# A two-part graph network on one core: loads of layer 2's counts in seven pieces, of the edge attributes in four, and an earlier first zero fill

## The chip, the core and the metric

One core of a Trainium2 chip runs the whole program. The metric is the time of the device in microseconds (us). The kernel before took 3525.62 us (median of three runs, 3514.42 to 3532.14).

## What is computed

There are 6250 nodes with 64 features and 206250 edges, sorted by destination. Two graph networks follow each other, each with a residual and a layer norm.

```python
def _sage_conv(x, src, dst, W_l, b_l, W_r):
    agg = segment_sum(x[src], dst) / maximum(count(dst), 1)[:, None]
    return agg @ W_l + b_l + x @ W_r
# first network
h = relu(_sage_conv(x, src, dst, W_l1, b_l1, W_r1))
h = relu(_sage_conv(h, src, dst, W_l2, b_l2, W_r2))
x = layernorm(x + h @ W_out + b_out)
# second network
m = selu(concat([x[src], edge_attr], 1) @ W1a + b1a) @ W1b + b1b
mean = segment_sum(m, dst) / maximum(count(dst), 1)[:, None]
x = layernorm(x + selu(concat([x, mean, u[0]], 1) @ W2a + b2a) @ W2b + b2b)
```

## The kernel before

The engines work side by side. Each has its own list of instructions, and semaphores tie the lists together: an instruction or a transfer raises one when it is done, and a `wait_ge` holds up everything behind it in the same list. The transfers that SP starts go out in the order of SP's list.

**Layer 1, about 0 to 670 us.** The nodes are cut into 14 superblocks of 448. For each of them TensorE and VectorE build the matrix of edge counts from every source (49 blocks of 128) to the 448 destinations, as 128 x 49 x 448 values of 16 bits, in one of the two halves of `A_sb`. TensorE multiplies the features with it, and SP stores it in DRAM (`A_d`, 5488 KB each, line 564). SP also fills the rows of `sorted_edges` with zeros, in eight pieces called `blank(r)` (lines 566 to 569, 1716 KB each), one behind each of the superblocks 4 to 11 (lines 576 to 579). The weights are loaded near the start (lines 534 to 547). The vector `zrow` of zeros is set by GpSimd in its first instructions.

**Layer 2, about 670 to 1280 us.** TensorE's `sums2(s)` (line 1408) computes the sums for one superblock from the counts and the stored features of layer 1: a product with zeros (line 1411) that opens the sum, a wait for the counts (line 1415), then seven bodies of 21 products (line 1435), each followed by one step `layer2(m, b)` of the superblock before it (line 1445). The steps are, in this order: turning the old features (`hT_turned`) and the product with `Wl2`; the product with `Wr2` (`v2_ready`); turning the new features (`h2_turned`); the product with `Wout` (`o_ready`); nothing; turning the normalised rows; and the last products (`pq_ready`). After the bodies 1, 3 and 6 there is also one small step of a sort (`place_group`). `agg2_ready` is raised by the last product of body 6, ahead of that body's `layer2` step. The counts of superblocks 12 and 13 are still on the chip when layer 2 begins, so `sums2(0)` and `sums2(1)` use those. The others, `sums2(2)` to `sums2(13)`, use twelve matrices that SP loads back, alternately into the two halves of `A_sb`.

SP's part is `superblock2(s)` (line 615):

```python
def superblock2(s, half, at_before=None):
    sp.wait_ge(agg2_ready, s)
    if s < NSB - 1:
        sp.dma_start(A_sb[:, 1 - half, :], A_d[...s - 1...]).then_inc(A_in[1 - half], 16)   # L618
    sp.wait_ge(x2_ready, s + 1)
    ...load_hx(s, half)                                                                    # L607, L608
    sp.wait_ge(p_ready, s)
    sp.dma_start(by_node(p_d, ...), pc[:, :, :]).then_inc(p_stored, 16)                    # L626
```

So the load in `superblock2(s)` is for `sums2(s + 1)`, and `p_ready` is raised to `s` by VectorE's last instruction for the superblock that `sums2(s)` carries with it (line 1944), which reads what TensorE wrote just ahead of `sums2(s + 1)`.

Between the bodies the first 40 groups of 1024 edges are sorted: ScalarE's queue loads them (`load_group`, lines 1062 to 1070), VectorE finds their places (`sort_group`, `slot_group`), and GpSimd writes their rows to `sorted_edges` with eight indirect transfers a group (line 890).

**The edges, about 1280 to 3526 us.** The other 162 groups go through the network in their own order. For group `h`, SP loads the attributes (`load_attr`, line 701, 256 KB, one of six buffers, 128 partitions of 2 KB), GpSimd gathers the source terms with eight indirect transfers (line 915), TensorE turns the attributes (`turn_attr`, line 1513, transposes of line 1519), multiplies them (line 1527) and sums the messages (line 1535), and VectorE and ScalarE compute the selu between them. Mixed in are 104 units of 512 sorted edges. SP loads a unit with two transfers (`load_unit`, lines 715 and 716), and TensorE turns it (`turn_unit`, line 1538, last transpose of line 1545). SP's list has the unit's two loads directly behind a `load_attr`, and `turn_unit` comes one group later in TensorE's list than the `turn_attr` for which that `load_attr` waited.

Of the kernel before, what the change touches and what calls it, by code (L numbers as in the profile page):

```python
# [7 lines left out]
F32 = mybir.dt.float32  # L8
# [8 lines left out]
P = 128  # L17
N = 6250
E = 206250
F = 64  # L20
# [23 lines left out]
SBN = SB_GROUPS * GROUP  # L44
NSB = 14
PAIRS = NSB // 2
BODIES = 7
BG = SB_GROUPS // BODIES
BH = SRC_BLOCKS // BODIES
# [9 lines left out]
EG = 1024  # L59
# [3 lines left out]
WIN = 48  # L63
RING = 3
DEEP = 6

RG = 5
NR = 8
PG = RG * NR
NEGC = NEG - PG  # L70
# [27 lines left out]
CELL_TILES = [cell_tiles(r) for r in range(NR)]  # L98
# [54 lines left out]
def build(nc, x, src, dst, edge_attr, Wl1, bl1, Wr1, Wl2, bl2, Wr2, Wout, bout,  # L153
# [8 lines left out]
    A_d = dram("counts_matrix", [NSB, P, SRC_BLOCKS * SBN], FP16)  # L162
# [6 lines left out]
    sorted_d = dram("sorted_edges", [NTILES * P + PRING * EG, F + 2], F32)  # L169

    with ExitStack() as ctx:
# [10 lines left out]
        A_sb = sb("A_sb", [P, 2, SRC_BLOCKS * SBN], FP16)  # L182
# [44 lines left out]
        zrow = sb("zrow", [P, 512], BF16)  # L227
# [163 lines left out]
        iota_set = sem("iota_set")  # L391
# [90 lines left out]
        def by_node(t, m):  # L482

            return t[bass.ds(m * SBN, SBN), :].rearrange("(c q) f -> q c f", q=CH)
# [34 lines left out]
        def _(sp):  # L519
# [26 lines left out]
            for half in range(2):  # L546
                sp.dma_start(Wedge[half * F:(half + 1) * F, half * F:(half + 1) * F], W1a[F:2 * F, :]).then_inc(w2_in, 16)

            def store_h(m, half):
                sp.wait_ge(h_split, m + 1)  # L550
                sp.dma_start(by_node(h1_d, m), hs[:, :, :]).then_inc(h_stored, 16)
                for part in range(3):
                    sp.dma_start(by_node(hp_d[part], m), hpart[:, part, :, :]).then_inc(h_stored, 16)
# [9 lines left out]
                sp.wait_ge(counts_moved, (s + 1) * SB_GROUPS + 2)  # L563
                sp.dma_start(A_d[bass.ds(s, 1), :, :].rearrange("a p n -> (a p) n"), A_sb[:, half, :]).then_inc(A_stored[half], 16)

            def blank(r):
                n, top = sum(CELL_TILES[r]), sum(sum(t) for t in CELL_TILES[:r])
                sp.dma_start(sorted_d[top * P:(top + n) * P, :].rearrange("(p t) f -> p (t f)", p=P).rearrange("p (t f) -> p t f", f=2 * (F + 2)),
                             zrow[:, 0:4 * (F + 2)].bitcast(F32).unsqueeze(1).to_broadcast([P, n // 2, 2 * (F + 2)])).then_inc(pm_blank, 16)

            for s in range(4):
                superblock(s, s % 2)
            sp.wait_ge(iota_set, 10)
# [1 line left out]
                sp.dma_start(pm_dst[:, :], dst[0:PG * EG].rearrange("(r q) -> r q", q=RG * EG)[:, 0].partition_broadcast(P)).then_inc(pm_dst_in, 16)  # L575
            for s in range(4, NSB):
                superblock(s, s % 2)
                if s - 4 < NR:
                    blank(s - 4)
            sp.wait_ge(xT_ready, NSB - 2)  # L580

# [30 lines left out]
            sp.wait_ge(A_stored[0], 16 * PAIRS)  # L612
            sp.wait_ge(A_stored[1], 16 * PAIRS)

            def superblock2(s, half, at_before=None):
                sp.wait_ge(agg2_ready, s)
                if s < NSB - 1:
                    sp.dma_start(A_sb[:, 1 - half, :], A_d[bass.ds(s - 1, 1), :, :].rearrange("a p n -> (a p) n")).then_inc(A_in[1 - half], 16)  # L618
                sp.wait_ge(x2_ready, s + 1)
                if isinstance(s, int) and s == 1:  # L620
                    sp.dma_start(h1m[1][:, :, :], by_node(h1_d, NSB - 1)).then_inc(hx_in[1], 16)
                    last_rows(xm[:, 1], hx_in[1])
                else:
                    load_hx(s, half)
                sp.wait_ge(p_ready, s)
                sp.dma_start(by_node(p_d, s - 3 if at_before is None else at_before), pc[:, :, :]).then_inc(p_stored, 16)  # L626

            superblock2(1, 1, NSB - 2)
            superblock2(2, 0, NSB - 1)
# [71 lines left out]
            def load_attr(h):  # L701
                g, k = PG + h, h % DEEP
                if h >= DEEP:
                    sp.wait_ge(attr_turned, h - DEEP + 1)
                if g < gE:
                    sp.dma_start(attr[k], edge_attr[g * EG:(g + 1) * EG, :].rearrange("(p j) f -> p (j f)", p=P)).then_inc(attr_in[k], 16)
                    return
                sp.dma_start(attr[k][0:ETAIL // EJ, :], edge_attr[te:te + ETAIL // EJ * EJ, :].rearrange("(p j) f -> p (j f)", j=EJ)).then_inc(attr_in[k], 16)
                sp.dma_start(attr[k][ETAIL // EJ:ETAIL // EJ + 1, 0:ETAIL % EJ * F], edge_attr[te + ETAIL // EJ * EJ:E, :].rearrange("(p j) f -> p (j f)", p=1)).then_inc(attr_in[k], 16)
# [528 lines left out]
        def _(pe):  # L1238
# [169 lines left out]
            def sums2(s, half, m=None):  # L1408
                if s > 0:
                    pe.wait_ge(agg2_moved, s)  # L1410
                pe.matmul(agg_ps[:, 0:SBN], zrow[:, 0:P], zrow[:, 0:SBN], start=True, stop=False, skip_group_check=True)
                if s < 2:
                    pe.wait_ge(counts_moved, NSB * SB_GROUPS + 2)
                else:
                    pe.wait_ge(A_in[half], s // 2 * 16)
                if s == 0:

                    for part in (2, 0, 1):
                        pe.wait_ge(part_in[part], 16)
                        for blk in range(EARLY):  # L1420
                            pe.matmul(agg_ps[:, 0:SBN], Hsb[:, part, blk, :], Asb(half)[:, blk, :], start=False, stop=True, skip_group_check=True)
                        if part == 0:
                            place_group(0)
                    pe.wait_ge(parts_in, 48)
                    for blk in range(EARLY, SRC_BLOCKS):
                        for part in range(3):
                            ins = pe.matmul(agg_ps[:, 0:SBN], Hsb[:, part, blk, :], Asb(half)[:, blk, :], start=False, stop=True, skip_group_check=True)
                    ins.then_inc(agg2_ready, 1)
                    return
                for b in range(BODIES):  # L1430
                    if s == NSB - 1 and b == BODIES - 1:
                        turn_last()
                    for blk in range(b * BH, (b + 1) * BH):
                        for part in range(3):
                            ins = pe.matmul(agg_ps[:, 0:SBN], Hsb[:, part, blk, :], Asb(half)[:, blk, :], start=False,  # L1435
                                            stop=(part == 2), skip_group_check=True)
                    if b == BODIES - 1:
                        ins.then_inc(agg2_ready, 1)
                    if s == NSB - 1 and b == BODIES - 1:
                        last_terms()  # L1440
                    layer2(m, b, 1 - half)
                    if b in (1, 3, 6):
                        place_group(3 * s - BEFORE + (1, 3, 6).index(b))
# [68 lines left out]

            def turn_attr(h):
                k = h % DEEP
                pe.wait_ge(attr_in[k], 16 * (h // DEEP + 1) + (16 if h == NEGC - 1 else 0))
                if h >= 1:
                    pe.wait_ge(attr_moved, h)
                for c in range(EJ // 2):
                    ins = pe.transpose(t_ps[:, c * P:(c + 1) * P], attr[k][:, c * P:(c + 1) * P], ident[:, :])  # L1519
                ins.then_inc(attr_turned, 1)  # L1520
# [707 lines left out]
```

## Time and profile before

| | |
|---|---|
| median of 3 runs | 3525.62 us |
| the profiled execution's own time | 3528.27 us |
| its span, first to last instruction | 3526.4 us |
| mean granted clock of TensorE, share of full | 0.768 |
| TensorE (PE), products | 2255.4 us busy, 64% |
| GpSimd (POOL) | 1785.5 us busy, 51% |
| VectorE (DVE) | 1420.1 us busy, 40% |
| ScalarE (ACT) | 962.0 us busy, 27% |

The page shows one execution. A busy share is the mean over stages that are bound differently, so the stages have to be read one at a time. "Landing" is the time from a transfer's issue to the semaphore that tells of its end. A wait put down to "remote" or to "another core or an unknown queue" is one whose releaser the profile couldn't name; there is one core here.

### The profile page before, as it was taken

The page shows a single profiled execution, that of the slowest core. Times are in us where ns is not written, and L with a number is a line of the kernel's source. Part 1 is how long each engine was busy: PE and PEld are TensorE (multiplying, and loading weights), DVE is VectorE, ACT ScalarE, POOL GpSimd, SP SyncE. Part 2 cuts the span into 40 slices and gives each one's busy share as a digit, 9 for nine tenths or more (in the row PEclk, how much of TensorE's full clock was granted, in tenths as well). Part 3 has the DMA queues.
Part 4 walks back from the last instruction along what each step waited for, and adds up shares of the span by engine and source line. Part 5 has one row for each costly group of instructions (what it writes and reads, how often), then busy time and mean ns, then how long its engine had stood idle before and what let it go on. Part 6 is the DMA issues. An engine that isn't in the chain of part 4 may idle for free.

```text
span 3526.4 us, 49813 instructions
## 1 busy us (share of the span) xinstructions
PE 2255.4 (64%) x17118; PEld 1609.5 (46%) x17118; DVE 1420.1 (40%) x2775; ACT 962.0 (27%) x2094; POOL 1785.5 (51%) x1840
## 2 busy tenths in 40 slices
PE   1799999888888851556556645555565555553543
PEld 1456555444444431444445444444544444443533
DVE  5698888143333340333323323232332323231323
ACT  2677777100000021222212212122222212221222
POOL 6233222155555556555555555555555555555562
PEclk9999999989988965676667767667666766665566
DMA  6346776678454411322212212222122222221111
GB/s 226 142 151 203 221 224 184 184 154 234 167 175 168 145 58 43 86 45 51 47 41 49 50 41 50 44 49 47 45 49 45 49 47 46 48 47 39 39 39 33
DMA packets 408743, 335.34 MB, mean 95 GB/s; under 512 B 296503, under 2 KB 357256, under 8 KB 404859
## 3 DMA queue, kind: packets, MB, share of 16 engines
q1 hardware_dynamic: 299249, 262.08, 25.2%
q0 software_dynamic: 54368, 57.24, 7.1%
q10 hardware_dynamic: 54922, 13.25, 1.8%
q8 instruction: 134, 2.20, 0.3%
q14 instruction: 70, 0.57, 0.1%
HBM read 199.25 MB, written 133.06 MB: 94 GB/s over the span
## 4 chain that ended last, share of the span: by engine, by line
PE 39%; another core or an unknown queue 29%; issue 18%; ACT 4%; DVE 4%; DMA 2%; SPq 1%; POOL 1%; DVEq 1%; ACTq 0%; POOLq 0%
PE agg_ps L1435 5%; PE cnt_ps L1306 5%; PE cnt_ps L1527 4%; PE agg_ps L1312 4%; PE agg_ps L1313 4%; PE u_ps L1566 3%; PE agg_ps L1576 3%; PE agg_ps L1535 3%; PE u_ps L1562 2%; PE t_ps L1519 2%; DMA overlapping_rows<-A_sb 1%; POOL A_sb L915 1%; SPq L637 1%; ACT A_sb L1137 1%
## 5 line engine op out<-in xcount | busy, mean ns | idle before, releaser
L915 POOL DMA_INDIRECT A_sb<-source_terms,src_cur x1296 | 1242.1, 958 | 950.9 <-ACT src_cur L1125 580.7
L1535 PE MATMUL agg_ps<-A_sb 128*65 128x48 f32 x2592 | 267.2, 253 | 361.4 <-issue 285.4
L1748 DVE TENSOR_TENSOR arena<-iota_code,arena 128x2048 f16<-128x2048 f16 (+1 forms) x392 | 435.8, 1178 | 79.9 <-PE cnt_ps L1306 67.4
L890 POOL DMA_INDIRECT sorted_edges<-pm_row,pm_to x320 | 315.0, 984 | 299.6 <-DVE pm_to L1898 210.1
L1435 PE MATMUL agg_ps<-A_sb,arena 128*128 128x448 f16 x1911 | 410.0, 367 | 43.3 <-issue 40.5
L1535 PEld LDWEIGHTS agg_ps<-A_sb 128*65 128x65 f32 x2592 | 244.1, 172 | 402.7 <-issue 314.4
L1010 ACT ACTIVATE A_sb<-cnt_ps 128x392 f32 (+1 forms) x784 | 385.7, 497 | 151.7 <-PE cnt_ps L1306 79.7
L1527 PE MATMUL cnt_ps<-Wedge,A_sb 128*128 128x128 f32 x1296 | 278.5, 363 | 176.3 <-issue 129.8
L1158 ACT ACTIVATE A_sb<-u_ps 128x256 f32<-128x256 f32 x104 | 40.1, 385 | 1072.1 <-remote 769.3
L1527 PEld LDWEIGHTS cnt_ps<-Wedge,A_sb 128*128 128x128 f32 x1296 | 235.1, 261 | 200.7 <-issue 153.4
L1566 PE MATMUL u_ps<-arena 128*128 128x64 bf16 x2472 | 172.6, 211 | 232.5 <-issue 231.7
L2055 DVE TENSOR_TENSOR A_sb<-A_sb,agg_ps 65x48 f32 (+1 forms) x266 | 67.8, 255 | 604.9 <-remote 452.9
L1306 PE MATMUL cnt_ps<-arena 128*128 128x98 f16 x3136 | 282.0, 214 | 42.6 <-ACT A_sb L1010 30.4
L1435 PEld LDWEIGHTS agg_ps<-A_sb,arena 128*128 128x128 bf16 x1911 | 188.8, 101 | 236.0 <-issue 90.8
L1306 PEld LDWEIGHTS cnt_ps<-arena 128*128 128x128 f16 x3136 | 189.5, 101 | 230.8 <-issue 183.3
L1566 PEld LDWEIGHTS u_ps<-arena 128*128 128x128 bf16 x2472 | 140.8, 111 | 253.7 <-issue 247.8
L1131 ACT ACTIVATE A_sb<-t_ps 128x512 f32<-128x512 f32 x162 | 96.4, 595 | 556.7 <-remote 385.6
L1313 PE MATMUL agg_ps<-A_sb,arena 128*65 128x448 f16 x686 | 243.9, 356 | 0.0
L1312 PE MATMUL agg_ps<-A_sb,arena 128*128 128x448 f16 x686 | 243.5, 355 | 0.2 <-ACT A_sb L1010 0.2
L2078 DVE SCALAR_TENSOR_TENSOR A_sb<-u_ps,A_sb 128x256 f32<-128x256 f32 x104 | 43.9, 422 | 446.9 <-ACT A_sb L1160 399.9
L2037 DVE TENSOR_TENSOR cnt_ps<-cnt_ps,A_sb 128x512 f32<-128x512 f32 x162 | 112.0, 691 | 120.9 <-remote 113.9
L817 POOL DMA_INDIRECT arena<-overlapping_rows,start_row x26 | 38.6, 1483 | 221.7 <-DVEq L1725 217.3
(295 smaller groups left out, 3222.4 us busy)
## 6 DMA issues: line engine op xcount, KB each, us to landing
counts_matrix<-A_sb SPq DMA_DIRECT2D x14, 5488.0 KB, 16.4
A_sb<-counts_matrix SPq DMA_DIRECT2D x12, 5488.0 KB
arena<-in_edge_attr_dram SPq DMA_DIRECT2D x107, 256.0 KB
A_sb<-source_terms,src_cur POOLq DMA_INDIRECT x1296
A_sb<-in_edge_attr_dram SPq DMA_DIRECT2D x54, 256.0 KB
sorted_edges<-zrow SPq DMA_DIRECT2D x8, 1716.0 KB, 25.2
arena<-sorted_edges SPq DMA_DIRECT2D x104, 128.0 KB
overlapping_rows<-A_sb SPq DMA_DIRECT2D x1, 13056.0 KB
```

The lines of the kernel that those rows point to most:

```text
L890: pool.indirect_dma_start(out=sorted_d, out_offset=bass.IndirectOffsetOnAxis(ap=pm_to[:, k, j:j + 1], axis=0), in_=pm_row[:, k, j, :], in_ ...
L915: pool.indirect_dma_start(out=gath[k][:, j * F:(j + 1) * F], out_offset=None, in_=p_d, in_offset=bass.IndirectOffsetOnAxis(ap=src_cur[k][: ...
L1010: act.activation(Asb(half)[:, :, bass.ds((b * BG + k) * GROUP, GROUP)].rearrange("p b (w j) -> p b w j", j=PAIR), cnt_ps[k % 2][:, 0:SUB * ...
L1306: ins = pe.matmul(cnt_ps[k % 2][:, c * CODES:(c + 1) * CODES], lane_hot[:, at + c // 2, :, c % 2], code_hot[:, at + c // 2, :, c % 2], sta ...
L1312: pe.matmul(agg_ps[:, 0:SBN], X12[:, blk, :], rhs, start=(blk == 0), stop=(blk == SRC_BLOCKS - 1), skip_group_check=True)
L1313: ins = pe.matmul(agg3_ps[0:F + 1, 0:SBN], X3[:, blk, :], rhs, start=(blk == 0), stop=(blk == SRC_BLOCKS - 1), skip_group_check=True)
L1435: ins = pe.matmul(agg_ps[:, 0:SBN], Hsb[:, part, blk, :], Asb(half)[:, blk, :], start=False, stop=(part == 2), skip_group_check=True)
L1527: ins = pe.matmul(cnt_ps[h % 2][:, c * P:(c + 1) * P], attrT[h % RING][:, c * P:(c + 1) * P], Wedge[:, :], start=True, stop=True)
L1535: ins = pe.matmul(agg3_ps[0:F + 1, 0:WIN], msg[h % RING][:, j, :], hot[h % RING][:, j, :], start=(j == 0), stop=(j == EJ - 1))
L1566: ins = pe.matmul(u_ps[:, j * F:(j + 1) * F], lane_p[u % 2][:, a, j * P:(j + 1) * P], P3[:, 2 * b + a, part, :], start=False, stop=(part = ...
L1748: ins = dve.tensor_tensor(hot_rows[:, slots], iota_code[:, 0:n, :].unsqueeze(1).to_broadcast([P, AT_ONCE * SUB // 2, n, 2]), turned[:, bas ...
L2037: dve.tensor_tensor(cnt_ps[h % 2][:, 0:EJ * F], cnt_ps[h % 2][:, 0:EJ * F], gath[h % DEEP], ALU.add).then_inc(z_made, 1)
```

## The change

Three things are changed. SP's load of a counts matrix becomes seven transfers of 784 KB (49/7 = 7 source blocks each). Piece 0 stands where the whole load stood, and pieces 1 to 6 stand behind the store of line 626, each of them behind a wait for the piece before it (`16 * i` on `A_in`) and in groups behind waits for `hT_turned`, `v2_ready`, `h2_turned` and `o_ready`. TensorE waits for all seven. The load of a group's attributes becomes four transfers of 32 partitions (64 KB); from the seventh group on each waits for the one before it. The first zero fill moves from behind superblock 4 to behind the weights.

```diff
+QUARTERS = 4
+QP = P // QUARTERS
+A_PARTS = BODIES
...
             for half in range(2):
                 sp.dma_start(Wedge[half * F:(half + 1) * F, half * F:(half + 1) * F], W1a[F:2 * F, :]).then_inc(w2_in, 16)
+            def blank(r):
+                ...
+            sp.wait_ge(iota_set, 10)
+            blank(0)
...
             for s in range(4, NSB):
                 superblock(s, s % 2)
-                if s - 4 < NR:
+                if 1 <= s - 4 < NR:
                     blank(s - 4)
...
+            def load_counts(s, half, i):
+                if s == NSB - 1:
+                    return
+                if i > 0:
+                    sp.wait_ge(A_in[half], 16 * A_PARTS * ((s - 1) // 2) + 16 * i)
+                cols = slice(i * BH * SBN, (i + 1) * BH * SBN)
+                sp.dma_start(A_sb[:, half, cols], A_d[s - 1, :, cols]).then_inc(A_in[half], 16)
+
             def superblock2(s, half, at_before=None):
                 sp.wait_ge(agg2_ready, s)
-                if s < NSB - 1:
-                    sp.dma_start(A_sb[:, 1 - half, :], A_d[bass.ds(s - 1, 1), :, :].rearrange("a p n -> (a p) n")).then_inc(A_in[1 - half], 16)
+                load_counts(s, 1 - half, 0)
                 sp.wait_ge(x2_ready, s + 1)
...
                 sp.wait_ge(p_ready, s)
                 sp.dma_start(by_node(p_d, s - 3 if at_before is None else at_before), pc[:, :, :]).then_inc(p_stored, 16)
+                sp.wait_ge(hT_turned, s)
+                load_counts(s, 1 - half, 1)
+                load_counts(s, 1 - half, 2)
+                sp.wait_ge(v2_ready, s)
+                load_counts(s, 1 - half, 3)
+                sp.wait_ge(h2_turned, s)
+                load_counts(s, 1 - half, 4)
+                load_counts(s, 1 - half, 5)
+                sp.wait_ge(o_ready, s)
+                load_counts(s, 1 - half, 6)
...
                 if g < gE:
-                    sp.dma_start(attr[k], edge_attr[g * EG:(g + 1) * EG, :].rearrange("(p j) f -> p (j f)", p=P)).then_inc(attr_in[k], 16)
+                    whole_rows = edge_attr[g * EG:(g + 1) * EG, :].rearrange("(p j) f -> p (j f)", p=P)
+                    for q in range(QUARTERS):
+                        if q > 0 and h >= DEEP:
+                            sp.wait_ge(attr_in[k], 16 * QUARTERS * (h // DEEP) + 16 * q)
+                        sp.dma_start(attr[k][q * QP:(q + 1) * QP, :], whole_rows[q * QP:(q + 1) * QP, :]).then_inc(attr_in[k], 16)
                     return
...
-                    pe.wait_ge(A_in[half], s // 2 * 16)
+                    pe.wait_ge(A_in[half], s // 2 * 16 * A_PARTS)
...
-                pe.wait_ge(attr_in[k], 16 * (h // DEEP + 1) + (16 if h == NEGC - 1 else 0))
+                pe.wait_ge(attr_in[k], 16 * QUARTERS * (h // DEEP) + 16 * (2 if h == NEGC - 1 else QUARTERS))
```

## Rows read from the trace of the kernel before

**Rows 1.** Busy time by stretch, in us: start:end length, then each engine's busy time.

```profile
957.50:1002.00 44.50, 36.64 (x199) 20.50 (x198) 17.31 (x57) 2.77 (x6) 23.60 (x24) 0.88 0.51 174
...
1500.00:3150.00 1650.00, 944.44 (x7523) 770.99 (x7522) 512.83 (x969) 363.37 (x868) 914.73 (x959) 0.69 0.21 47
```

**Rows 2.** Timeline of SP's queue in layer 2: start us, us, line, transfer.

```profile
696.51 0.37 SPq L618 DMA_DIRECT2D A_sb<-counts_matrix  x1
...
731.12 0.33 SPq L626 DMA_DIRECT2D source_terms<-iota_i  x1
731.49 0.49 SPq L618 DMA_DIRECT2D A_sb<-counts_matrix  x1
...
1002.41 0.33 SPq L626 DMA_DIRECT2D source_terms<-iota_i  x1
1002.78 0.49 SPq L618 DMA_DIRECT2D A_sb<-counts_matrix  x1
...
1220.45 0.33 SPq L626 DMA_DIRECT2D source_terms<-iota_i  x1
```

**Rows 3.** Timeline of TensorE where two superblocks of layer 2 begin.

```profile
827.90 2.42 PE L1435 MATMUL agg_ps<-A_sb,arena 128*128 128x448 f16 x6 [2.12 <-DMA A_sb<-counts_matrix]
...
1001.60 0.53 PE L1411 MATMUL agg_ps<-zrow 128*128 128x448 bf16 x1
...
1001.92 5.60 PE L1435 MATMUL agg_ps<-A_sb,arena 128*128 128x448 f16 x21
```

**Rows 4.** Chain that ended last, at the one load of counts on it.

```profile
810.87 16.67 DMA A_sb<-counts_matrix
```

**Rows 5.** DMA issues of the page: count, KB each, median us to landing.

```profile
counts_matrix<-A_sb SPq DMA_DIRECT2D x14, 5488.0 KB, 16.4
...
sorted_edges<-zrow SPq DMA_DIRECT2D x8, 1716.0 KB, 25.2
...
h_rows<-hs SPq DMA_DIRECT2D x14, 224.0 KB, 2.6
...
out_dram<-arena SPq DMA_DIRECT2D x13, 112.0 KB, 2.3
...
out_dram<-arena SPq DMA_DIRECT2D x1, 84.0 KB, 1.8
```

**Rows 6.** Timeline at the start: a load of 803.2 KB and the instruction it releases.

```profile
2.30 0.45 SPq L521 DMA_DIRECT2D A_sb<-in_dst_dram  x1
...
7.20 0.25 DVE L1682 CAST A_sb<-A_sb 128x102 int16<-128x102 int32 x1 [5.70 <-DMA A_sb<-in_dst_dram]
```

**Rows 7.** Timeline of GpSimd and ScalarE in one superblock of layer 2.

```profile
995.64 0.97 POOL L890 DMA_INDIRECT sorted_edges<-pm_row,pm_to  x1 [0.30 <-issue]
998.96 0.54 ACT L1085 ACTIVATE agg3S<-cnt_ps 64x448 f32<-64x448 f32 x1 [16.70 <-remote]
...
1009.36 6.97 ACTq L1070 DMA_DIRECT2D pm_ends<-in_dst_dram  x1
...
1020.12 0.97 POOL L890 DMA_INDIRECT sorted_edges<-pm_row,pm_to  x1 [5.26 <-DVE pm_to L1898]
```

**Rows 8.** Timeline of the edges, SP's queue: loads of a group and of a unit.

```profile
1961.94 0.35 SPq L706 DMA_DIRECT2D arena<-in_edge_attr_dram  x1
1962.33 0.43 SPq L715 DMA_DIRECT2D arena<-sorted_edges  x1
1962.81 0.51 SPq L716 DMA_DIRECT2D arena<-sorted_edges  x1
...
2015.62 0.35 SPq L706 DMA_DIRECT2D arena<-in_edge_attr_dram  x1
```

**Rows 9.** The same stretch: TensorE's turning of units, and ScalarE's waits.

```profile
1968.75 0.27 PE L1545 MATMUL t_ps<-ident,arena 128*8 128x128 f32 x1
...
1976.61 2.08 PE L1527 MATMUL cnt_ps<-Wedge,A_sb 128*128 128x128 f32 x8 [5.40 <-issue]
...
2023.19 0.27 PE L1545 MATMUL t_ps<-ident,arena 128*8 128x128 f32 x1
...
2043.35 0.39 ACT L1158 ACTIVATE A_sb<-u_ps 128x256 f32<-128x256 f32 x1 [16.78 <-PE u_ps L1566]
```

**Rows 10.** Timeline near 74 us: the last weights, and the gathers behind them.

```profile
71.66 2.22 SPq L547 DMA_DIRECT2D Wedge<-in_L_gnn_W1a_dram  x2
...
100.40 0.94 POOL L801 DMA_INDIRECT arena<-first_dst,part_of  x1 [0.30 <-issue]
...
104.54 0.89 ACT L1010 ACTIVATE A_sb<-cnt_ps 128x392 f32 x2 [4.47 <-remote]
```

More of the change, by code:

```diff
@@ L547, in _ @@
                 sp.dma_start(Wedge[half * F:(half + 1) * F, half * F:(half + 1) * F], W1a[F:2 * F, :]).then_inc(w2_in, 16)
+            def blank(r):
+                n, top = sum(CELL_TILES[r]), sum(sum(t) for t in CELL_TILES[:r])
+                sp.dma_start(sorted_d[top * P:(top + n) * P, :].rearrange("(p t) f -> p (t f)", p=P).rearrange("p (t f) -> p t f", f=2 * (F + 2)),
+                             zrow[:, 0:4 * (F + 2)].bitcast(F32).unsqueeze(1).to_broadcast([P, n // 2, 2 * (F + 2)])).then_inc(pm_blank, 16)
+            sp.wait_ge(iota_set, 10)
+            blank(0)
             def store_h(m, half):
@@ L564, in superblock @@
                 sp.dma_start(A_d[bass.ds(s, 1), :, :].rearrange("a p n -> (a p) n"), A_sb[:, half, :]).then_inc(A_stored[half], 16)
[L566 to L569, printed above, removed]
             for s in range(4):
```

## The prediction

> **What bounds the kernel now.** I first read the busy time by stretch. No engine is full in either of the stages that the change touches. One superblock of layer 2 takes 44.5 us with TensorE busy for 36.6 and GpSimd for 23.6, and in the 1650 us of the edges TensorE is busy for 944 and GpSimd for 915 [rows 1]. So each stage is a loop of waits, and what counts is which wait ends last.
>
> In layer 2 the load of the counts is not that wait. SP issues it within 1.2 us of the start of a superblock: line 626, behind which it stands, goes out at 1002.41, the load at 1002.78, and TensorE opened the sums at 1001.60 [rows 2, 3]. It lands about 16.7 us later [rows 4] and is needed only at the next superblock, some 44 us on. What costs time there is elsewhere: ScalarE sits idle for 16.7 us, until just after GpSimd has written the last of a run of 16 row transfers [rows 7]. The edges show the same picture, with ScalarE idle for 16.8 us at a time [rows 9]. Only once is a load of counts waited for, for 2.12 us at 827.90 [rows 3], where it had been queued behind the long index loads.
>
> **Layer 2, the term that decides.** The seven pieces would have to be on the chip before `sums2(s + 1)` begins. Piece 0 is: it keeps the old place. Pieces 1 to 6 stand behind SP's wait for `p_ready` at `s`. That semaphore is raised when superblock `s` is completely done, and the rows show when this is: line 626, the first thing behind the wait, goes out at 1002.41, while TensorE's first product that needs counts ran at 1001.92 [rows 2, 3]. So pieces 1 to 6 begin 0.5 us after the moment at which all seven are wanted. The four new waits (`hT_turned`, `v2_ready`, `h2_turned`, `o_ready`) spread nothing, because each asks for a step of `sums2(s)`, and all of these came before `p_ready`. They cost nothing either. Nothing else can be in front: the matrix that was loaded in the 44 us of cover now has one seventh of its load in that cover.
>
> What remains is six transfers, one after the other, since each waits for the landing of the one before. The price of one (784 KB): a transfer of 224 KB lands in 2.6 us [rows 5] and one of 5488 KB in 16.67 [rows 4]. On the line between them 784 KB takes 2.6 + 560 x (16.67 - 2.6)/5264 = 4.1 us. I add 0.1 for SP to wake and issue the next, and take 4.2. The bounds are 2.6 (the smaller transfer) from below and 4.9 from above, from the load of 803.2 KB issued at 2.30 that releases VectorE at 7.20, next to another load of its size [rows 6]. I choose near the upper one because its size is nearly the same.
>
> The Trainium skill's page "DMA: Bandwidth & Descriptors", section "Anatomy of one DMA — SWDGE (gpsimd) path", puts one transfer at about 2.0 us plus its bytes over 436 GB/s, which would make a piece 3.8 us, an estimate from that page; its section "Bandwidth" tells to batch transfers to 1 MiB or more, which speaks against cutting this load. With 3.8 in place of 4.2 the sum below would be 29 us less.
>
> Per superblock: SP's store of line 626 and the gap, 0.37; six pieces, 25.2; and 0.49 from TensorE's first product to line 626. That is 26.1 us in which TensorE stands still. VectorE and ScalarE soon stand as well, since their steps hang on products of the same superblock, and GpSimd has one group of eight writes to do (some 10 us) and then waits. Nothing covers it. It comes 12 times, for `sums2(2)` to `sums2(13)`: line 626 goes out 12 times between 731.12 and 1220.45 [rows 2]. 12 x 26.1 = 313 us. The wait of 2.12 us at 827.90 [rows 3] is inside it, so 311. With the bounds of the piece it is 196 to 361.
>
> What comes back? Piece-wise loading lets other queues in between. In the trace an issue of ScalarE's queue took 6.97 us while the whole matrix was loading [rows 7]. But the places that GpSimd waits for at 1020.12 come from VectorE [rows 7], behind TensorE's bodies, so the writes start no earlier. I book nothing, and keep 0 to 40 us for the range.
>
> **The edges.** TensorE waits for the attributes of a group that were asked for six groups earlier, so the four quarters themselves are hidden. What is queued behind them is not: a unit's two loads. Today they go out 0.4 and 0.9 us behind line 706 [rows 8]. Three waits for landings come in front of them. A quarter is 64 KB; the nearest transfers are 84 KB in 1.8 us and 112 KB in 2.3 [rows 5]. I take 2.1 for each, so the unit's loads leave 6.4 us later (5.4 to 6.9). SP's second load then leaves 7.3 us behind line 706 and lands some 3 us after, 10.3 in all. TensorE wanted the unit of 1961.94 at 1968.75, after 6.8 us, and that of 2015.62 at 2023.19, after 7.6 [rows 8, 9]: 3.5 and 2.7 us too late. These are the tight ones of the six turned in those 90 us. If every lateness counted, it would be (3.5 + 2.7)/6 x 104 = 107 us. But just there TensorE or ScalarE stands anyway: TensorE for 5.4 us until 1976.61 and ScalarE for 16.8 until 2043.35 [rows 9], and these end with GpSimd's runs of transfers, not with the unit. I book 20, with 0 and 107 as the ends and perhaps 20 gained, if TensorE's pauses let the others catch up.
>
> SP can keep up: about 7 us of its list per group against 13.8 us for a group (the stage of some 2240 us over 162). The 18 extra issues at the start of the stage (0.35 us each) lie beside 48 gathers.
>
> **The first zero fill.** It leaves at 73.9 and lands 25.2 us later [rows 5, 10], beside GpSimd's gathers until 100.40, behind which ScalarE gets on at 104.54 [rows 10]. These are on the path. If each of the 18 gathers lost a few tenths, it is 3 us (0 to 15). Behind superblock 4 it was beside other work, and its absence gains nothing.
>
> **Sum.** 3528.3 (the profiled execution's own time, 2.7 above the median) + 311 + 20 + 3 = 3862, or about 3860 against the median of 3525.6. That is 9.5% slower.
>
> **The rivals.**
> 1. *The late units count in full.* Every group is a loop through all engines, and a unit that comes late holds up the next `attr_product`. For it: TensorE's order has no slack behind `turn_unit`. Against it: the standing times above. Time: 3860 + 87 = 3947. Chance 0.17.
> 2. *The scatter gets out of the way.* TensorE's 26 us of standing still let GpSimd finish its writes, so that ScalarE's 16.7 us at the end of each superblock go. This would give 12 x 16.7 = 200 back: 3660. Against it: two of the three groups of writes need places that are found after bodies 1 and 3. Chance 0.09.
> 3. *The other side: faster.* The standing times of 16.7 us (layer 2) and 16.8 us (edges) are made by large transfers in the way of small ones, and the smaller pieces end them. Place: ScalarE's waits in rows 7 and 9. Price: at least 3 us gained in each of 162 groups, 486 us, against 314 lost in layer 2: 3350. It decides from 2 us a group. Against it: in the edges the attribute load is only 256 KB, and ScalarE's wait ends with GpSimd's run, not with a landing. Chance 0.04. The same page's section "Queues, rings and completion order" says that an engine takes turns between queues packet by packet; by that rule smaller rows would help the small transfers, which is this rival.
> 4. *The change doesn't do what I read.* If `p_ready` came early enough in some way, the pieces would be hidden and only the edges change: within 0.5%, which is about what a measurement of this kernel can tell. The rows put line 626 behind TensorE's start each time, so 0.02.
>
> My forecast has 0.68. **The range.** With the piece between 2.6 and 4.9, what comes back and the late units, the likeliest case covers 3705 to 4000. The far low end needs a piece of 784 KB as quick as one of 224 KB, so I begin at 3755; at the top I include rival 1 with a slightly dearer piece: 4020. Chances: faster 0.04, same 0.02, slower 0.94.
>
> **What would show it.** In SP's queue after the change, line 626's successor should be followed by six issues about 4.2 us apart, and TensorE should wait some 26 us for "DMA A_sb<-counts_matrix" twelve times, with superblocks of about 70 us; the clock granted to TensorE should stand at its lower level when it resumes. In the edges the issues of the unit loads should stand about 7 us behind the first quarter, with short waits at line 1545's successor and a stage about as long as now (2245 us). I am wrong if the pieces show up ahead of TensorE's start, if superblocks stay under 60 us, or if the edges' stage moves by over 60 us.

## The result, and the profile after the change

The changed kernel took 3854.93 us (median of four runs, 3852.81 to 3860.36) against 3525.8 for the one before on the same chip. The ratio is 1.094 (95% interval 1.0909 to 1.097), so it is 9.4% slower. The profiled execution took 3852.81 us, its span is 3851.0 and the mean granted clock 0.747.

The products of layer 2 in the page before, then in the page after with the loads of counts. Their busy time is as before, and what is new is the idle time ahead of them:

```profile
L1435 PE MATMUL agg_ps<-A_sb,arena 128*128 128x448 f16 x1911 | 410.0, 367 | 43.3 <-issue 40.5
...
L1462 PE MATMUL agg_ps<-A_sb,arena 128*128 128x448 f16 x1911 | 411.4, 368 | 356.9 <-DMA A_sb<-counts_matrix 321.3
...
A_sb<-counts_matrix SPq DMA_DIRECT2D x84, 784.0 KB
```

SP's queue in layer 2 after, at the superblock that answers to [rows 2] (start us, us, line, transfer; neighbours of one line are grouped, with the time from the first to the last):

```profile
699.36 0.37 SPq L627 DMA_DIRECT2D A_sb<-counts_matrix  x1
...
741.37 0.33 SPq L639 DMA_DIRECT2D source_terms<-iota_i  x1
...
1018.78 0.33 SPq L639 DMA_DIRECT2D source_terms<-iota_i  x1
1019.21 23.91 SPq L627 DMA_DIRECT2D A_sb<-counts_matrix  x7
...
1593.72 0.33 SPq L669 DMA_DIRECT2D source_terms<-iota_i  x1
```

TensorE at the same place, which answers to [rows 3], and ScalarE at the end of that superblock and of the next, which answers to [rows 7]:

```profile
1018.64 0.56 PE L1438 MATMUL agg_ps<-zrow 128*128 128x448 bf16 x1 [0.53 <-ACT aggS L1123]
1046.65 6.83 PE L1462 MATMUL agg_ps<-A_sb,arena 128*128 128x448 f16 x21 [27.45 <-DMA A_sb<-counts_matrix]
...
1054.58 4.14 PE L1462 MATMUL agg_ps<-A_sb,arena 128*128 128x448 f16 x21
```

```profile
1016.25 0.54 ACT L1112 ACTIVATE agg3S<-cnt_ps 64x448 f32<-64x448 f32 x1 [15.06 <-remote]
...
1053.90 0.54 ACT L1102 ACTIVATE xTs<-t_ps 128x448 f32<-128x448 f32 x1 [35.31 <-PE t_ps L1480]
...
1087.12 0.54 ACT L1112 ACTIVATE agg3S<-cnt_ps 64x448 f32<-64x448 f32 x1 [15.05 <-remote]
```

Line 639, the old line 626, goes out at 1018.78, 0.14 us behind TensorE's opening product. The old load for this superblock would have been on the chip by then. Now SP sends six pieces and the first of the next matrix within 23.91 us, and TensorE's first product that needs counts comes at 1046.65. ScalarE then waits 35.31 us for TensorE. The 21 products behind the wait take 6.83 us, and the 21 of the next body 4.14.

The waits of the whole execution (us in total, times, longest):

```profile
PE agg_ps L1462 <- DMA A_sb<-counts_matrix: 321.3, 12, 27.6
PE t_ps L1571 <- DMA arena<-sorted_edges: 108.8, 55, 6.6
```

Busy time by stretch, one superblock and the edges, which answers to [rows 1]:

```profile
1018.64:1087.84 69.20, 36.75 (x189) 19.09 (x190) 16.67 (x54) 2.11 (x5) 23.44 (x24) 0.76 0.36 109
...
2000.00:3600.00 1600.00, 905.99 (x7042) 729.93 (x7041) 477.35 (x906) 344.64 (x816) 882.78 (x928) 0.69 0.22 46
```

The superblock has the same work (TensorE 36.75 us, GpSimd 23.44) in 69.2 us instead of 44.5. The edges look as they did: TensorE busy for 57% of the stretch both times.

**Where the 325 us are**, from the two profiled executions (3851.0 - 3526.4 = 324.6):

| stretch | before | after | more |
|---|---|---|---|
| to the first load of layer 2 | 696.51 | 699.36 | 2.9 |
| from there to the last store of `p` | 587.4 | 894.4 | 307.0 |
| from the first attribute load to the end | 2240.7 | 2255.5 | 14.8 |

Within layer 2 TensorE waits 12 times for the counts, 321.3 us in all or 26.8 each, where it waited 2.1 us before: 319 more. The twelve superblocks to which these waits belong, from the store at 731.12 (741.37 after) to the last one, grew by 300 together, 25.0 each. So some 19 us came back. They are found in TensorE's other pauses of this stretch, which add up to 93 us in the trace before and 75 in the one after: the pauses ahead of the products that follow ScalarE's stand (line 1483, now 1510) went from 32.1 to 22.5, those between the products of the sums from 40.5 to 31.8. ScalarE's stand at the end of a superblock did become shorter, from 16.70 us [rows 7] to 15.06 and 15.05, but that isn't the account of it: two of the stands before were shorter than that (5.0 and 12.1 us), and over the twelve superblocks they add up to 181 us before and 177 after. What made the pauses shorter is not shown.

The stretch from the first load to the first store, behind which the first late pieces go out, grew by another 7.4 us, from 34.6 (696.51 to 731.12) to 42.0 (699.36 to 741.37). `sums2(1)` took 40.7 us in it instead of 33.0. This is not shown to be the change's doing: in the traces of e2 and e3 below, whose layer 2 is that of the kernel before, it takes 40.6 and 39.2.

In the edges the quarters go out one landing after the other, and the unit's loads behind them:

```profile
2315.77 7.43 SPq L733 DMA_DIRECT2D A_sb<-in_edge_attr_dram  x4
2323.25 0.42 SPq L742 DMA_DIRECT2D arena<-sorted_edges  x1
...
2329.88 5.61 SPq L733 DMA_DIRECT2D arena<-in_edge_attr_dram  x4
2335.53 0.43 SPq L742 DMA_DIRECT2D arena<-sorted_edges  x1
```

```profile
2325.88 0.44 PE L1571 MATMUL t_ps<-ident,arena 128*128 128x128 f32 x2 [0.30 <-DMA arena<-sorted_edges]
...
2338.53 0.44 PE L1571 MATMUL t_ps<-ident,arena 128*128 128x128 f32 x2 [1.85 <-DMA arena<-sorted_edges]
```

The unit's first load leaves 7.5 and 5.7 us behind the first quarter instead of 0.4 [rows 8], and TensorE waits for it 55 times, 108.8 us in all; before, no such wait showed.

### The profile page after: what moved, and what is told of

Same layout as the page of the kernel before. It is cut to its first block, busy times and chain, and to the rows that moved or that the text cites. A ratio compares the mean times of both kernels' runs of the same rounds, so it can differ in the third digit from the quotient of the medians.

```text
span 3851.0 us, 50418 instructions
## 1 busy us (share of the span) xinstructions
PE 2297.6 (60%) x17118; PEld 1632.8 (42%) x17118; DVE 1420.1 (37%) x2775; ACT 962.3 (25%) x2094; POOL 1771.4 (46%) x1840
## 4 chain that ended last, share of the span: by engine, by line
PE 30%; another core or an unknown queue 24%; issue 20%; DMA 16%; SPq 3%; ACT 3%; DVE 3%; ACTq 0%; DVEq 0%; POOL 0%; POOLq 0%
DMA A_sb<-counts_matrix 7%; PE agg_ps L1462 6%; PE cnt_ps L1333 4%; DMA arena<-in_edge_attr_dram 4%; PE agg_ps L1339 3%; PE agg_ps L1340 3%; DMA A_sb<-in_edge_attr_dram 2%; PE agg_ps L1562 2%; PE cnt_ps L1554 2%; PE u_ps L1593 2%; SPq L733 2%; PE agg_ps L1603 1%; DMA arena<-sorted_edges 1%; DMA overlapping_rows<-A_sb 1%
## 5 line engine op out<-in xcount | busy, mean ns | idle before, releaser
L1462 PE MATMUL agg_ps<-A_sb,arena 128*128 128x448 f16 x1911 | 411.4, 368 | 356.9 <-DMA A_sb<-counts_matrix 321.3
L1562 PEld LDWEIGHTS agg_ps<-A_sb 128*65 128x65 f32 x2592 | 255.2, 184 | 312.0 <-issue 260.9
L1945 DVE TENSOR_TENSOR ht<-u_ps,inv_c 112x512 f32<-112x512 f32 x14 | 9.7, 692 | 380.5 <-PE u_ps L1484 380.5
```

The lines of the kernel that those rows point to most:

```text
L1562: ins = pe.matmul(agg3_ps[0:F + 1, 0:WIN], msg[h % RING][:, j, :], hot[h % RING][:, j, :], start=(j == 0), stop=(j == EJ - 1))
```

## The experiments

The same kernel before took 3579.7 us on the chip of the first four runs (`e1` to `e4`) and 2828.1 and 2827.3 us where the other eight ran. Each ratio is against runs of the kernel before beside it, and a size is carried from one of these chips to another only where the text says so. The last section comes back to this.

**e1: the pieces alone.** The edges and the zero fill are as before.

```diff
-                    for q in range(QUARTERS):
-                        ...
+                    sp.dma_start(attr[k], ...whole...).then_inc(attr_in[k], 16)
...
-            blank(0)
+                if s - 4 < NR:
+                    blank(s - 4)
```

> Only the counts of layer 2 come in seven pieces; attributes and zero fill as before. Theory (six pieces stand behind the end of the superblock and land one by one): nearly the whole loss, 305 us more than before, within 10, with TensorE waiting for the counts 12 times for 26 to 27 us (321 us in the changed kernel). Rival (late units or the zero fill carry a good part of it): under 290 us more.

It took 3876.19 us, a ratio of 1.0838 (1.081 to 1.0867), 296.5 us more. TensorE's wait is the one of the full change:

```profile
PE agg_ps L1456 <- DMA A_sb<-counts_matrix: 324.5, 12, 27.5
```

That is some nine tenths of the 329 us that the full change cost, if a size may be carried from one chip to the other. The 305 us within 10 that I expected were just met.

**e2: the quarters alone**, in the kernel before.

```diff
-                    sp.dma_start(attr[k], ...).then_inc(attr_in[k], 16)
+                    for q in range(QUARTERS):
+                        if q > 0 and h >= DEEP:
+                            sp.wait_ge(attr_in[k], ...)
+                        sp.dma_start(attr[k][q * QP:(q + 1) * QP, :], ...).then_inc(attr_in[k], 16)
```

> Only the attributes come in quarters that wait for each other. Theory (the units come late, but where the engines stand anyway): 10 to 20 us more than before (the stage of the edges grew by 15 us in the changed kernel), with some 109 us of TensorE's waits for units. Rival (the lateness counts in full): 60 us or more. Rival (noise): within 5 us.

3605.06 us, ratio 1.0064 (1.0044 to 1.0085), 25.4 us more, above the 10 to 20 that I expected. TensorE waits for units about as long as in the full change, and the time grows by about a fifth of that:

```profile
PE t_ps L1550 <- DMA arena<-sorted_edges: 113.6, 54, 7.2
```

**e3: the zero fill alone.**

```diff
+            sp.wait_ge(iota_set, 10)
+            blank(0)
...
-                if s - 4 < NR:
+                if 1 <= s - 4 < NR:
```

> Only the first zero fill leaves behind the weights. Theory (it slows the gathers of the start a little and gives nothing back later): 0 to 5 us more than before, layer 1 ending 3 us later as in the changed kernel. Rival (it relieves superblock 4): 3 us or more less than before.

3575.55 us, ratio 0.9987 (0.9973 to 1.0002). The interval holds no change, so the fill costs nothing in the end at its new place. Whether it delays layer 1 stays open. The first load of layer 2 leaves at 695.37 here and at 691.49, 693.70 and 692.46 in e1, e2 and e4 beside it, 1.7 to 3.9 us later, and after the full change it left 2.9 later than before. But e7 and e8, which leave layer 1 alone and ran on one chip, have it at 686.08 and 694.62. The 2.9 us stay unassigned.

**e4: the pieces where they are covered.** As e1, but pieces 1 to 6 with their four waits stand ahead of the wait for `p_ready`.

```diff
+                sp.wait_ge(hT_turned, s)
+                load_counts(s, 1 - half, 1)
+                ...
+                sp.wait_ge(o_ready, s)
+                load_counts(s, 1 - half, 6)
                 sp.wait_ge(p_ready, s)
                 sp.dma_start(by_node(p_d, ...), pc[:, :, :]).then_inc(p_stored, 16)
```

> As the first of these kernels, but the pieces 1 to 6 and their four waits stand ahead of SP's wait for p_ready, so that they leave while the superblock before is being computed. Theory (place is the whole fault): the time of before within 10 us, no wait of TensorE for counts over 3 us, superblocks of 44 us. Rival (small pieces let the other queues through and end the idle 16.7 us of ScalarE): 50 to 200 us less than before. Rival (seven serial landings are too slow even there): 50 us or more above before.

3598.04 us, ratio 1.0045 (1.0025 to 1.0065): 18.4 us more instead of 296.5. I had expected at most 10 and no wait over 3 us. SP's queue and TensorE, where the one wait is left:

```profile
740.91 23.55 SPq L625 DMA_DIRECT2D A_sb<-counts_matrix  x6
779.42 0.33 SPq L647 DMA_DIRECT2D source_terms<-iota_i  x1
...
780.34 15.42 SPq L658 DMA_DIRECT2D arena<-in_src_dram  x1
...
797.40 15.21 SPq L658 DMA_DIRECT2D arena<-in_dst_dram  x1
...
814.55 0.38 SPq L625 DMA_DIRECT2D A_sb<-counts_matrix  x1
...
820.37 22.79 SPq L625 DMA_DIRECT2D A_sb<-counts_matrix  x6
```

```profile
847.36 3.17 PE L1456 MATMUL agg_ps<-A_sb,arena 128*128 128x448 f16 x8 [22.72 <-DMA A_sb<-counts_matrix]
```

The six transfers and their four waits are the same as in e1. Only their place behind `p_ready` is gone, and 278 of the 296 us go with it. What is left is one superblock of 63.8 us from store to store (779.42 to 843.20), where the first profile of before has 49.3 (774.83 to 824.16): its pieces are queued behind the two long index loads, where the whole matrix had just squeezed through (a wait of 2.12 us, [rows 3]). The other superblocks have 45 us. In them ScalarE's stand is not ended by the smaller pieces:

```profile
975.93 0.54 ACT L1106 ACTIVATE agg3S<-cnt_ps 64x448 f32<-64x448 f32 x1 [16.84 <-remote]
```

That takes the ground from rival 3, by which smaller pieces end these stands. The profile of before could have told as much: the load of the superblock that began at 957.50 [rows 1] leaves within 1.2 us and lands 16.7 us on, at about 975, and ScalarE's stand that ends at 998.96 [rows 7] begins at 982.26.

**e5: one late transfer instead of six.** As e1 with two parts: piece 0 at the old place, and the other 4704 KB in one transfer behind `p_ready`. **e6: seven pieces, not paced.** As e1, but no piece waits for the one before it.

```diff
-            A_PARTS = BODIES
+            A_PARTS = 2                      (e5)
...
-                if i > 0:
-                    sp.wait_ge(A_in[half], 16 * A_PARTS * ((s - 1) // 2) + 16 * i)   (e6)
```

> Counts only: piece 0 in its place, pieces 1 to 6 as one transfer of 4704 KB behind the store of p. This keeps the late place and takes the serial landings away. Theory (place and serial landings add up): such a transfer lands in some 14.5 us, TensorE waits 12 times for 15 to 16 us, and the time is 175 to 195 us above before. Rival (the place alone makes the loss): near the 297 us of the seven pieces. Rival (the serial landings alone make it): within 20 us of before.

> Counts only, seven pieces in the late place, but no piece waits for the one before. Theory (landings are what costs, not the number of transfers): as the one late piece, TensorE's waits 15 to 17 us each, 175 to 205 us above before. Rival (the number of transfers costs): over 250 us above before.

e5: 3027.13 us, ratio 1.0705 (1.0683 to 1.0726), 199 us more, a little above what I expected. e6: 3025.28 us, ratio 1.0698 (1.0677 to 1.072), 197 us more. The waits of e5, then of e6:

```profile
PE agg_ps L1448 <- DMA A_sb<-counts_matrix: 195.2, 12, 21.4
```

```profile
PE agg_ps L1454 <- DMA A_sb<-counts_matrix: 196.1, 12, 17.4
```

One transfer or six make no difference (16.3 us a wait in both). So the cut itself costs nothing, and neither do six issues of some 0.5 us. What the two have in common is the place: 16.3 us of waiting a superblock. What e1 has more is that each piece waits for the landing of the one before: 27.0 us a wait, 10.7 more, or 128 us over twelve; in the times of the whole kernel the difference is 98 us (296.5 against 197 to 199). It is between runs on different chips, so neither number is shown as cleanly as the rest: e1 was not run beside e5 and e6. But a whole matrix lands no faster on theirs, 18.2 us in the median of e9's page against 16.67 [rows 4]:

```profile
A_sb<-counts_matrix SPq DMA_DIRECT2D x12, 5488.0 KB, 18.2
```

**e7 and e8: which part of the quarters costs.** e7 takes away the waits between the quarters, e8 keeps them and issues a unit's loads ahead of the quarters. **e9 and e10** repeat e2 and e8 beside each other.

```diff
-                        if q > 0 and h >= DEEP:
-                            sp.wait_ge(attr_in[k], ...)          (e7)
...
+                for unit in UNIT_LOADS[h]:
+                    load_unit(unit)
                 if h >= DEEP:
                     load_attr(h)
-                for unit in UNIT_LOADS[h]:
-                    load_unit(unit)                              (e8, e10)
```

> Attributes only, in quarters, issued at once without waits for landings. Theory (the waits in front of the unit loads make the 25 us of the quarters): within 8 us of before, and TensorE's waits for units nearly gone. Rival (four small transfers are dearer than one): 15 us or more above before.

> Attributes only, in quarters with their waits, but SP issues a unit's two loads ahead of the group's quarters. Theory (the late units make the 25 us): within 8 us of before, TensorE's waits for units under 10 us in total. Rival (it is the waiting of SP or the quarters themselves): 15 us or more above before.

> The quarters with their waits once more, next to the following kernel and whatever time before has here. Theory: where before takes about 3550 us (idle stretches of 16 to 20 us of ScalarE) the late units cost 0.4 to 0.9%; where it takes about 2830 us they cost under 1% too, since GpSimd's gathers bound the stage. Rival (their cost in the second job came from something else): within 0.2% of before.

> The units' loads ahead of the quarters, next to the quarters as they were. Theory (late units are the cost): faster than the kernel of the quarters run beside it, and within 0.3% of before. Rival: as slow as the quarters run beside it.

| | us | ratio | 95% |
|---|---|---|---|
| e7 | 2829.82 | 1.0007 | 0.9997 to 1.0018 |
| e8 | 2829.36 | 1.0001 | 0.999 to 1.0011 |
| e9, as e2 | 2827.39 | 1.0 | 0.999 to 1.001 |
| e10, as e8 | 2829.69 | 1.0009 | 0.9994 to 1.0023 |

Here the quarters cost nothing in any form, e2's own included. That is e9's rival (within 0.2% of before), and e10 is no faster than e9. The waits of TensorE for units, in e9 and then in e10:

```profile
PE t_ps L1550 <- DMA arena<-sorted_edges: 118.6, 35, 25.3
```

```profile
PE t_ps L1550 <- DMA arena<-sorted_edges: 50.3, 8, 20.6
```

e7 has no such wait, and e8 has 9 of them, 47.6 us in all, where I had expected under 10. So the waits between the quarters and the order of SP's list do decide how long TensorE waits for units. But on this chip 118.6 us of it is free, because the stage hangs on GpSimd, which does its gathers of e9 with hardly a stop:

```profile
L921 POOL DMA_INDIRECT A_sb<-source_terms,src_cur x1296 | 1242.9, 959 | 398.1 <-issue 396.4
```

Whether the late units are what costs 25 us on e2's chip is therefore not shown. These four runs gave no answer to it, as they ran where there is nothing to explain.

**e11: the index loads later.** The kernel before, with the two long index loads and their neighbours moved from behind superblock 2 to behind the loads of superblock 12.

```diff
-            ... six index loads and two of base_i, behind superblock2(2)
+            def load_ends(): ...the same...
...
                     load_hx(s, half)
+                if s == NSB - 2:
+                    load_ends()
```

> The kernel before, with whole loads of counts, but the long loads of sources and destinations moved from ahead of the fourth load of counts to behind the last one. Theory (those loads hold up one load of counts): the one wait for counts goes, 2 to 7 us less where before takes about 3550 us and 15 to 20 us less where it takes about 2830. Rival (they hold up what stands at the end of layer 2 in its place): no gain, or a loss up to 30 us.

2802.48 us, ratio 0.9907 (0.9891 to 0.9924): 24.8 us less than the kernel before beside it, and more than the 15 to 20 that I expected. The changed kernel was not run on this chip. The wait that went, here as e9 has it, whose layer 2 is that of the kernel before:

```profile
809.65 6.93 PE L1441 MATMUL agg_ps<-A_sb,arena 128*128 128x448 f16 x21 [22.54 <-DMA A_sb<-counts_matrix]
```

In e11 no product of layer 2 waits for counts. With the 22.5 us go the 2.8 by which the 21 products behind the wait are slower (6.93 against 4.14), 25.3 in sum. At its new place the first long load holds SP for 33.36 us, beside work:

```profile
1060.86 33.36 SPq L623 DMA_DIRECT2D arena<-in_src_dram  x1
...
1096.19 15.09 SPq L623 DMA_DIRECT2D arena<-in_dst_dram  x1
```

**e12: both moves.** e4 with the index loads behind the last pieces of superblock 12.

```diff
                 load_counts(s, 1 - half, 6)
+                if s == NSB - 2:
+                    load_ends()
                 sp.wait_ge(p_ready, s)
```

> The seven pieces of counts ahead of the wait for p_ready, with those index loads moved behind the last pieces. Theory (the pieces ahead cost their 18 us at one superblock alone, where they queue behind the index loads): within 0.3% of the kernel with whole loads and index loads later, run beside it. Rival (pieces in the right place cost in each superblock): 10 us or more above it.

2852.21 us, ratio 1.0089 (1.0072 to 1.0106), 49.7 us more than e11 beside it. The expectation missed. Its SP queue and TensorE:

```profile
867.11 0.33 SPq L663 DMA_DIRECT2D source_terms<-iota_i  x1
...
873.50 28.05 SPq L625 DMA_DIRECT2D A_sb<-counts_matrix  x6
901.73 0.33 SPq L663 DMA_DIRECT2D source_terms<-iota_i  x1
```

```profile
900.91 0.35 PE L1436 MATMUL agg_ps<-zrow 128*128 128x448 bf16 x1
...
905.96 6.78 PE L1460 MATMUL agg_ps<-A_sb,arena 128*128 128x448 f16 x21 [4.70 <-DMA A_sb<-counts_matrix]
```

The expectation rested on e4, where a superblock took 45 us. Here it takes 33.0 (e11), and the chain of the pieces no longer fits: it begins 6.4 us into the superblock (at 873.50, after the wait for `hT_turned`), and piece 6 goes out at the end of the 28.05 us and has still to land, when `sums2` has opened at 900.91. Eight such waits come to 25.5 us, each with slow products behind it. From 721.84 to 1086.19 ten superblocks take 364.4 us, 36.4 each instead of 33.0, which is 34 us. The end of layer 2 takes the rest: from the store at 1086.19 to that at 1169.28, 83.1 us pass, where e11 has 68.2 (1058.15 to 1126.32): the index loads begin 31.4 us behind that store, at 1117.62, and in e11 2.0 us behind it. So even ahead of `p_ready` the pieces cost 1.8% here. That is the price of the chain together with its late start behind `hT_turned`, 6 to 11 us into a superblock; the two were not tried apart. The three other waits hardly lengthen the chain: a step with one of them in it takes 4.8 us on average in this trace, a step without one 5.0.

## Why the prediction was right

**The ordering.** "Pieces 1 to 6 begin 0.5 us after the moment at which all seven are wanted": line 639 goes out 0.14 us behind TensorE's opening product, and the six follow. e4 shows that this step decides: the same pieces ahead of `p_ready` cost 18 us instead of 296.

**The price of a piece.** 4.2 us, plus 0.37 and 0.49 once, made 26.1 a superblock; TensorE's wait measures 26.8. The issues of pieces 3 to 6 of that superblock (the last row holds piece 6 and the first piece of the next matrix):

```profile
1028.61 0.33 SPq L627 DMA_DIRECT2D A_sb<-counts_matrix  x1
...
1033.61 0.33 SPq L627 DMA_DIRECT2D A_sb<-counts_matrix  x1
...
1037.96 0.33 SPq L627 DMA_DIRECT2D A_sb<-counts_matrix  x1
...
1042.31 0.81 SPq L627 DMA_DIRECT2D A_sb<-counts_matrix  x2
```

From piece 1 (1019.21) to piece 6 (1042.31) there are five steps of 4.6 us, and 4.3 to 4.5 on average in the eleven other superblocks; from the twelve waits it is 26.8/6 = 4.5 a piece. So the piece was sized 0.3 too low, and the 0.86 beside it too high, since it lies ahead of the wait: 12 x (6 x 0.27 - 0.86) = 9, the difference of 319 to my 311 within 1. The Trainium skill's page "DMA: Bandwidth & Descriptors", section "Anatomy of one DMA — SWDGE (gpsimd) path", gave an estimate of 3.8 a piece; its formula is stated for transfers that GpSimd issues, and these are SP's. The trace is farther from it than from the line through the rows.

**"Nothing covers it"** held, and the count of 12 too. Where I had 311 us the waits are 319. I booked nothing for what comes back (range 0 to 40), and some 19 came back in TensorE's other pauses. I had no term for the start of layer 2, where 7 were lost, and by e2 and e3 these may have nothing to do with the change. That layer 2 came out at 307 against 311 is luck in part, since these errors cancel.

**"Piece-wise loading lets other queues in between"** held too, in ScalarE's queue. In e4 the same issue that took 6.97 us beside a whole matrix [rows 7] goes out between the pieces in 0.96 us:

```profile
997.35 0.96 ACTq L1091 DMA_DIRECT2D pm_ends<-in_dst_dram  x1
```

It won no time, as I had booked it: e4 is slower than before, not faster.

**The edges.** 20 booked, 14.8 in the two traces, 25.4 in e2. TensorE did wait for late units, and most of it was absorbed. That the waits come to 108.8 us and my lateness to 107 is luck in part: I had carried two tight units of six over to all, some 35 units late by 3.1 us, and there are 55 waits of 2.0. Why 15 to 25 us are left is not shown.

**The zero fill.** 3 booked; e3 finds none in the whole time, and its interval ends at 0.02% more.

**The sum.** 3862 against 3852.8 for the profiled execution, and 3860 against the median 3854.9. The ends that I gave for the likeliest case, 3705 and 4000, don't come out of my terms. With 196 to 361 us for layer 2, 0 to 40 back, -20 to 107 in the edges and 0 to 15 for the fill it is 3664 to 4011. The result is far from either end.

**The rivals.** Rival 1 needed 87 us more in the edges than the 20 booked; there are 14.8 in the traces and 25 in e2. Rival 2 needed ScalarE's 16.7 us gone; 15.06 are left. Rival 3 fell with e4 (the stand is there without large transfers near it) and e2 (smaller attribute loads gained nothing). Rival 4 needed `p_ready` early; it isn't. I leaned on round robin between queues for rival 3, from the Trainium skill's page "DMA: Bandwidth & Descriptors", section "Queues, rings and completion order"; no run here shows that rule itself at work, and whether it holds is open. The shorter issue in ScalarE's queue fits it without showing it, and ScalarE's stands did not go with it.

**What I named as signs.** Six issues about 4 us apart, twelve waits of 26 to 28 us, superblocks of about 70 us (68.6 to 70.9, the last 74.7) and unit loads about 7 us behind the first quarter are all there. So is the lower clock at the restart: 6.83 us for 21 products, against 4.14 one body later. The granted clock stands at 0.50 of full when TensorE resumes, the lower of its two levels of 1.2 and 2.4 GHz, and at 1.00 eight microseconds on:

```profile
1046.00:1050.00 4.00, 3.35 (x10) 1.36 (x11) 0.00 (x0) 0.00 (x0) 0.00 (x0) 0.50 0.79 274
...
1054.00:1058.00 4.00, 4.00 (x26) 2.35 (x25) 0.69 (x1) 0.44 (x1) 0.00 (x0) 1.00 0.33 68
```

It adds less than it seems, since before the first 21 products took 5.60 us already [rows 3].

## What to carry to other kernels

Before a load is cut into pieces that are to hide behind the steps of an iteration, find where the end of that iteration stands in the queue's list: pieces behind that wait are behind all the work they were to hide in, whatever finer waits stand between them. A chain in which each piece waits for the landing of the one before needs more cover than the whole did, here 27 us against 16.7. And look for what stands ahead of a prefetch in its queue: two index loads of some 16 us each stood ahead of a load of counts, and where a superblock takes 33 us moving them gave 0.9%. Where it takes 44 the load was waited for only 2.1 us, so less is to be had there; that was not run.

## What was not expected

**The same kernel took 3525.8, 3579.7, 2828.1 and 2827.3 us** (medians of 4, 20, 19 and 19 runs, with spreads of 0.3 to 0.7%). I had taken the stands of 16.7 us for a property of the program. On the two chips of e5 to e12 they are absent: a superblock has 33.0 us instead of 44.5, and GpSimd's 1296 gathers wait for nothing but their own issue (the row of e9 above, 398.1 us idle), where the first profile of before has:

```profile
L915 POOL DMA_INDIRECT A_sb<-source_terms,src_cur x1296 | 1242.1, 958 | 950.9 <-ACT src_cur L1125 580.7 <-issue 370.0
```

The mean duration of a gather is the same, 958 and 959 ns. What differs is the others. In the slower traces TensorE falls to a few products at a time while GpSimd writes its rows, as here in the profile after, each burst 1.4 us behind the last, and ScalarE goes on 2 to 3 us after GpSimd's run ends (the last of it at 1013.38, ScalarE at 1016.25):

```profile
1010.45 0.92 PE L1462 MATMUL agg_ps<-A_sb,arena 128*128 128x448 f16 x4 [0.51 <-issue]
1011.88 0.92 PE L1462 MATMUL agg_ps<-A_sb,arena 128*128 128x448 f16 x4 [0.51 <-issue]
```

TensorE's clock is not what holds it there, although its mean over the whole run is lower before (0.768) than in e9 (0.826). In the stretch of these bursts it is granted in full:

```profile
1009.00:1013.00 4.00, 2.75 (x12) 1.15 (x12) 0.00 (x0) 0.00 (x0) 3.09 (x4) 1.00 0.08 25
```

What makes this on one occasion and not on the other, and whether it is the chip or something else of the occasion, was not tried and stays open. It goes with different verdicts, though: the quarters cost 0.6% where the stands exist and nothing where they don't, and pieces placed as in e4 fit into 45 us (but for the one superblock with the index loads) and, by e12, not into 33.
